# Constant mask rows of the attention stacks written from patterns four tiles wide, for both pairs of stacks in the period of sequence 0

## The reference

```python
xn = _layernorm(x)
s = attention(xn)          # 16 heads, causal softmax over 512 keys
g = silu(experts(xn))      # top 2 of 8
x = x + s * g
xn = _layernorm(x)
s = recurrence(xn)         # W = W - lr * (W k - v) k^T, y = W q
g = silu(xn @ sign(weight).T)
return x + s * g
```

## Time and profile before

| | us |
|---|---|
| median of 3 runs | 600.81 |
| lowest and highest run | 598.35 and 602.64 |
| the profiled execution's own time | 601.28 |
| its span, first to last instruction | 599.5 |
| PE busy in it | 568.1 (95%) |
| DVE, ACT, POOL busy | 397.5, 347.6, 178.4 |

### The profile page before, as it was taken

The page is one execution under the profiler, slowest core; times in us unless marked ns, Lnnn a source line. Parts: engine busy times, 40 slices in busy tenths (PEclk is TensorE's granted clock), DMA queues, the critical chain, the costliest instruction groups (busy, mean ns, idle before and its releaser), DMA issues.

```text
span 599.5 us, 17372 instructions
## 1 busy us (share of the span) xinstructions
PE 568.1 (95%) x7217; PEld 381.1 (64%) x7217; DVE 397.5 (66%) x983; ACT 347.6 (58%) x670; POOL 178.4 (30%) x353
## 2 busy tenths in 40 slices
PE   8789999899899999999999999999999999899797
PEld 3345575467666686677666776677677777565464
DVE  3478667576668876786868777777768676422553
ACT  3521556764568556765667466765676476676231
POOL 6356204222215322241314312432224201411221
PEclk9999999999999999999999999999999999899999
DMA  3767093749054202620143204520262100000001
GB/s 90 161 157 160 15 105 69 128 87 110 19 125 91 62 3 69 136 65 21 46 104 78 62 12 106 110 63 4 63 131 50 29 12 1 27 19 1 3 3 36
DMA packets 58161, 39.41 MB, mean 66 GB/s; under 512 B 17956, under 2 KB 57987, under 8 KB 58083
## 3 DMA queue, kind: packets, MB, share of 16 engines
q1 hardware_dynamic: 58051, 38.29, 31.5%
q10 hardware_dynamic: 32, 0.01, 0.0%
HBM read 24.46 MB, written 9.96 MB: 57 GB/s over the span
## 4 chain that ended last, share of the span: by engine, by line
PE 78%; ACT 9%; DVE 5%; POOL 3%; issue 3%; DMA 1%; SPq 0%; POOLq 0%; DVEq 0%
PE ps_v L963 12%; PE ps_s L944 11%; PE ps_e L925 7%; PE ps_a L879 5%; PE ps_a L865 4%; PE ps_c L1024 4%; PE ps_e L917 3%; PE ps_e L921 3%; PE ps_a L829 3%; PE ps_s L947 2%; PE ps_e L747 2%; ACT hid L1244 2%; ACT prob L1261 2%; PE ps_a L844 2%; PE ps_c L1006 2%
## 5 line engine op out<-in xcount | busy, mean ns | idle before, releaser
L1471 DVE TENSOR_REDUCE cand<-ps_s 128x4 f32<-128x512 f32 (+1 forms) x320 | 212.4, 685 | 51.1 <-PE ps_s L947 31.6
L1261 ACT ACTIVATE prob<-ps_e 128x512 f32<-128x512 f32 x320 | 187.2, 598 | 80.5 <-PE ps_e L925 54.5
L944 PE MATMUL ps_s<-kst,qst 72*128 72x128 bf16 (+2 forms) x1024 | 124.8, 234 | 6.2 <-DMA kst<-k_scratch 1.8
L944 PEld LDWEIGHTS ps_s<-kst,qst 72*128 72x128 bf16 (+1 forms) x1024 | 74.1, 98 | 66.9 <-DVE cand L1471 29.5
L925 PE MATMUL ps_e<-qst,kst 75*128 75x256 bf16 (+3 forms) x416 | 105.1, 284 | 0.0
L963 PE MATMUL ps_v<-prob,vaug 128*32 128x512 f32 (+3 forms) x1024 | 87.7, 443 | 0.0
L917 PE MATMUL ps_e<-identb,negmask 128*128 128x150 bf16 (+3 forms) x320 | 72.9, 228 | 4.1 <-ACT prob L1261 4.0
L921 PE MATMUL ps_e<-qst,kst 128*128 128x128 bf16 x384 | 74.6, 220 | 0.0
L925 PEld LDWEIGHTS ps_e<-qst,kst 75*128 75x128 bf16 x416 | 40.7, 98 | 3.6
L747 PE MATMUL ps_e<-identb 128*128 128x512 bf16 x115 | 40.6, 408 | 1.9 <-POOL identb L520 1.9
L917 PEld LDWEIGHTS ps_e<-identb,negmask 128*128 128x128 bf16 x320 | 31.2, 98 | 15.3 <-ACT prob L1261 11.2
(11 more groups left out here) (341 smaller groups left out, 903.5 us busy)
## 6 DMA issues: line engine op xcount, KB each, us to landing
qst<-q_scratch SPq DMA_DIRECT2D x48, 192.0 KB
kst<-k_scratch SPq DMA_DIRECT2D x48, 192.0 KB
q_scratch<-qparts SPq DMA_DIRECT2D x24, 128.0 KB, 2.3
k_scratch<-kparts SPq DMA_DIRECT2D x24, 128.0 KB, 2.3
x_res<-in_L_attn_x_dram SPq DMA_DIRECT2D x8, 256.0 KB, 3.2
xn<-in_L_attn_x_dram SPq DMA_DIRECT2D x7, 256.0 KB, 3.7
out_dram<-second SPq DMA_DIRECT2D x7, 256.0 KB, 2.5
max_scratch<-mrow SPq DMA_DIRECT2D x16, 96.0 KB, 2.0
```

What stands on the lines that cost most here:

```text
L944: last = mm(ps_s[:, bank, w * n:w * (n + 1)], q[0:rows, hd, tok(i)], k[0:rows, hd, keys[0]:keys[1]], start=(n == 0), stop=True, skip_group ...
L1261: af(prob[:, u, :], ps_e[:, u % 2, :], ACT.Exp).then_inc(S["e_emptied"], 1)
L1471: vec.tensor_reduce(cand[:, i, h0:h0 + FILLS * (len(hds) - 1) + 1:FILLS, S_SLOT[u]], ps_s[:, u % 2, :].rearrange("p (a c) -> p a c", a=len ...
```

## The change

`load_pads` no longer reads `identb` and `negmask`. POOL first writes, at the start of `masks`, two patterns that hold each of them four times side by side (128 x 512 in bf16, so a row is 1,024 bytes), into `body.sy`, a tile of layer 1 that has no other use until sequence 0 gets there. Each DMA then writes a row of source 16 times, once per head. SP waits for `masks_ready` at 1, which POOL gives at the end of `masks`. Both pairs are loaded behind `m_rows1` in the period of sequence 0, none in that of sequence 1.

```diff
+        pad_rows = body.sy.rearrange("p i d -> p (i d)").bitcast(BF16).rearrange("p (n q) -> p n q", n=2)
...
             def load_pads(p):
 
                 few = MROWS - EVEN
-                for st, of in ((qst[p], identb), (kst[p], negmask)):
+                sp.wait_ge(S["masks_ready"], 1)
+                for n, st in enumerate((qst[p], kst[p])):
                     for rows in (slice(few, MROWS), slice(0, few)):
-                        sp.dma_start(st[SROWS + rows.start:SROWS + rows.stop, :, :].rearrange("p h (i c) -> p (h i) c", c=P),
-                                     bcast(of[rows, :], 1, HEADS * NT)).then_inc(S[f"pads_loaded{p}"], 16)
+                        sp.dma_start(st[SROWS + rows.start:SROWS + rows.stop, :, :], bcast(pad_rows[rows, n, :], 1, HEADS))\
+                            .then_inc(S[f"pads_loaded{p}"], 16)
...
-                if half and b.c < 2:
-                    load_pads(b.parity)
+                if half and b.c == 0:
+                    for p in range(2):
+                        load_pads(p)
...
             def masks():
+                for n, of in enumerate((identb, negmask)):
+                    chain(g.tensor_copy(pad_rows[:, n, :].rearrange("p (i c) -> p i c", c=P), bcast(of[:, :], 1, NT)))
                 chain(g.memset(vaug[:, :, :, :], 0.0))
```

## The result

The changed kernel takes 605.29 us (median of 8 runs, 603.59 to 608.91) where the kernel before takes 599.27 (median of 8, 596.82 to 603.33): a ratio of 1.0101 with an interval from 1.006 to 1.0141. It is slower by 1%, 6 us. The forecast was 599.1; the time lies above the range, on the side of rival A.

The account below looks back on a forecast made before the run. PE, busy 95%, was taken as the bound, through its waits and matmul pace. 601.28 - 1.7 + 0 + 0 = 599.6; with that execution 0.47 us above the median, 599.1 was forecast, range 596.8 to 602.3.

Parts of the forecast that it names:

- rival A: Wide pads move no faster per byte, at 113 GB/s, and delay sequence 2's stacks by 8.6 us: 607.7; chance 0.07.
- the two gaps: PE's only waits without a releasing instruction: 1.7 us at 149.78 and 1.6 us ending at 116.47.
- the small gap: PE's 1.70 us wait inside 32 small matmuls, period of sequence 1; laid to an instruction packet some 3 us late.
- Part 1: No pads in the period of sequence 1: gain of 1.7 us, bounded by 1.70 and 2.42.
- Part 3: Two pattern copies on POOL, 1.2 to 2.3 us, fit into 5.22 us of idle time: cost 0.
- Part 2: Both pairs in the period of sequence 0: at 180 GB/s the pads end at 95.8, so cost 0.
- The sign that the prediction had named for being wrong: Sequence 2's writes, forecast to stay at 98.9, move; one of three signs that would prove the prediction wrong.
- the limit of 97.0: Latest end of the pads, in us, that leaves sequence 2's writes at 98.9; it needs 169 GB/s.
- Rival B: Nothing happens: the gap at 149.78 comes from PE's instruction supply and stays or moves; 600.8, chance 0.12.
- Rival C: The longer pads starve PE in the period of sequence 0: a new gap of 1.7 us, about 600.8; chance 0.03.
- the stack gap: PE's wait ahead of the first wide `s_unit` for sequence 2's stack load; 1.6 us before, forecast unchanged.

Follow-up runs that it names:

- e8: The kernel before, run again with no edit for a second trace; 604.16 us in its one run.
- e9: Against the kernel before: 256-byte rows kept, pair 1's pads some 14 us earlier, behind the load of sequence 3's input; 597.04 us, ratio 0.9961.
- e1: Against the changed kernel: wide rows kept, but each pair loaded in its old period; 597.94 us, ratio 0.9963 to the kernel before.
- e4: Against the changed kernel: pair 1 copied from pair 0's landed rows in pieces of 4,096 bytes, SP waiting for pair 0 first; 611.60 us in its one run.
- e6: Against the changed kernel: patterns first written to DRAM at 57.4 us, and the eight pad DMAs read them there; 607.39 us, ratio 1.0122.
- e2: Against the kernel before: narrow 256-byte rows kept, both pairs loaded in the period of sequence 0; 611.60 us, ratio 1.0196.
- e5: Against the changed kernel: each of the five odd rows in a DMA of its own, 16 more DMAs; 607.02 us, ratio 1.0122.
- e3: Against the changed kernel: pair 0's pads behind the load of sequence 2's input (about 58 us), pair 1 at about 76; 597.35 us, ratio 0.9968.
- e10: Against the changed kernel: wide rows, pair 0's pads at about 60 us and pair 1's at about 122; 598.12 us, ratio 0.9984.

## Why the prediction was wrong

**What bounds the kernel, the two gaps: right.** The difference lies in these two places (5.4 us, against 4.8 in all), and both depend on the pads as the prediction said. That the small gap is the pads' doing was argued from the packet's lateness; e8 shows that it comes again and e9 that it goes when nothing but the time of the pads is moved. The lateness was misread, though: "some 3 us" took 65.40 us, the length of the next period, as the distance to the twin, but the two runs of 32 lie 217.12 - 149.46 = 67.66 apart. The packet was due at about 143.0 and was 5.3 us late, and PE ran 182 instructions in 142.9 to 149.78, not 143, before it stopped; in e1, some 2.8 us late, it stopped nothing. What isn't shown is how the packet's arrival and the end of the gap hang together; the gap ends 3.2 (before) and 3.0 us (e8) after the packet starts.

**Part 1, a gain of 1.7, bounded by 1.70 and 2.42: right.** The period went from 67.82 to 65.91, 1.9 us. I had put 0.72 us of the excess down to the other matmuls of sequence 1; 0.5 us of it indeed stayed. What the term left out: the gap can bring the lower clock with it, as e8 shows, so the stretch was 1.9 us longer than the changed kernel's in one execution and 3.4 in the other (67.82 and 69.31 against 65.91). The sum also started high: the three runs behind it have a median of 600.81, the eight of the comparison 599.27. So the step that failed weighs more than the 6.2 us between forecast and result: a gain of 1.7 was forecast, a loss of 6.0 measured.

**Part 3, POOL at 0: right.** 0.61 us each, covered.

**Part 2 is the step that failed, in its choice of a rate.** It put the cost at zero, with the pads through at 95.8 by a rate of 180 GB/s; they were through at 104.57, and the gap grew by 6.90 us. The 180 came from the one row with SBUF on both sides. That row was 3 us long, held weight loads and writes to DRAM beside the 96 pieces of `ones_bf`, and so was hardly a row of such a transfer at all. The pads ran at 145, then 107 to 109, and at 114 over the whole; the cover, SP's wait for ACT until 98.9, would have needed 169 by the prediction's own working. The nearest rows were the pads' own, 132 and 106, for the same rows, partitions and engines; from them to the measured rates it is a factor of 1.0 to 1.1, from 180 it is one of 0.6 to 0.8. e4 shows that pieces of 4,096 bytes gain nothing over 1,024, e6 that the source matters little. The sign that the prediction had named for being wrong came: the writes of `q_scratch` moved, from 98.91 to 105.11.

The trace of the kernel before had the answer without any rate. Pair 0 alone, 1.74 MB, was landing until 95.48, 19.0 us after 76.5, or 92 GB/s. The 113 that the prediction called the pads' own mean (its two rows give 115) stops at 89, ahead of the tail:

```profile
89.00:95.50 6.50, 5.40 (x53) 3.52 (x51) 6.19 (x22) 4.58 (x9) 2.52 (x8) 1.00 0.50 53
```

So one pair was through only 1.5 us ahead of the limit of 97.0, and a second one was put behind it.

**Rival A was what happened, at 0.07.** Its mechanism was right. It said 607.7 and a delay of 8.6 us; measured are 605.3 and 6.9 us. Its end of the pads, 107.2, is nearly what came, 104.57 + 2.30 = 106.9 in the time of the kernel before, but by luck: 113 GB/s was neither the narrow pads' mean to their last landing (92) nor taken from wide ones (114 in e1 and in the changed kernel). Most of the 1.7 us by which it was too long is that it let SP's writes start 1.9 us behind the pads, with `max_scratch` still to go. That DMA had been issued at 92.22 and landed 0.17 us after the pads, and the writes started 0.54 us after them. The limit of 97.0, and with it the 169 GB/s, has the same 1.9 us in it, so the true limit is somewhat lower; no run lies near it. The rival spoke of the rate of bytes rather than of pieces. In fact both count, since the wide form alone took one pair from 92 to 114 GB/s to the last landing, or in the dense stretches from 115 (76.5 to 89) to 149 (e1), and halved the loss of the place (e2 against the changed kernel). The section of the Trainium skill that the rival was set beside, "Why small descriptors are slow (HBM only)" of "DMA: Bandwidth & Descriptors", says that transfers between SBUF and SBUF don't suffer from small descriptors. This case doesn't agree: with 256-byte pieces both pairs went at 110 GB/s in 75 to 96 (e2), with 1,024-byte pieces at 145 in 74.2 to 88. The gain is real and was less than the forecast needed.

**Rival B fell:** the small gap came in both traces with narrow pads in that place (e8) and went when they were moved (e9). **Rival C** didn't come up: no gap without a releaser before 112.55, though the instruction packet among the pads started at 99.8, where it was 95.7 in a trace whose first period was 2.30 us longer, so some 6.4 us late.

**The chances:** a limit at 169 GB/s, with 167 in one row, 180 in a mixed one, and 106 to 132 in the rows of the same transfer, is no case for 0.07. The range followed from it.

## What to carry to other kernels

When transfers are moved forward on a queue, work out the rate at which the whole lot runs empty from the rows of these very transfers, and ask which rate uses up the time until the next waited-for transfer; look also for the time at which the last piece of the same transfer landed, since a mean over its dense part leaves out the tail. A better form of the pieces is a guess until a run shows it. A load that nobody waits for still has a place in time: it costs what stands behind it on the queue, and it can hold up the instructions of the busiest engine. Here the form was worth 0.4% and the place cost 2% at the old form; a change that does both shows only the sum.

## What the runs showed of the hardware

- Constant rows into partitions 75 to 127 moved at 106 to 132 GB/s in pieces of 256 bytes (110 over 21 us in e2), at 145 to 150 in the first 9 to 14 us in pieces of 1,024 (e1, e4, the changed kernel), and at 147 in pieces of 4,096 (e4); at 129 with the source in DRAM (e6). While transfers into one partition each went, all DMA together moved 26 to 33 GB/s (e5).
- A gap of PE's instructions of 1.70 us, twice the same, when its 16 KB instruction packet started only 1.0 to 1.2 us before the run of matmuls that stopped (before, e8). None at a lead of 3.9 us, behind 1,024-byte pieces in the same place (e1), nor at 6.5 to 6.8 us, without pads (the changed kernel, e9).
- The clock behind the stack gap: at 1.00 throughout with gaps of 1.0 (e1), 1.2 (e3) and 1.4 us (e10), down to 0.50, 1.2 GHz, in every trace with 1.6 us and more, and also with 1.4 us in e9. With the same matmuls behind it, the stretch up to layer 1's first Gram matrices took 15.19 us in e3 and 16.70 in the kernel before:

```profile
115.90:131.09 15.19, 15.19 (x132) 9.92 (x133) 12.45 (x29) 10.83 (x18) 6.14 (x8) 1.00 0.60 109
```

```profile
116.47:133.17 16.70, 16.70 (x131) 10.98 (x132) 12.55 (x29) 10.50 (x18) 5.59 (x8) 0.90 0.57 98
```

So a stack gap that is 0.4 us shorter came with 1.9 us less in all, 1.5 of them by the clock. As e9 and e10 show, a gap of 1.4 us can come with the fall and without it; that executions of one kernel differ for this reason is likely and not shown.
